# Moving two attention context groups within the software pipeline of a macaron layer

## The reference

```python
x = x + 0.5 * ffn(layernorm(x), k0, k1, k2, s0, s1, s2)
x = x + attn(layernorm(x), Wq, bq, Wk, bk, Wv, bv, gamma, beta)
x = x + 0.5 * ffn(layernorm(x), k0, k1, k2, s0, s1, s2)

# ffn: three dense layers with weights of +1 or -1 (128 -> 512 -> 512 -> 128),
#      h = relu(s * (h @ w)) * 2 between them
# attn: 16 heads of 8 features, softmax over 256 keys,
#       layernorm(context + x) * gamma + beta
```

## Time and profile before

| | us |
|---|---|
| median of 3 runs | 710.48 |
| lowest and highest | 710.31, 711.82 |
| profiled execution | 712.18 |
| its span, first to last instruction | 710.4 |
| busy: TensorE, VectorE, ScalarE, GpSimd | 672.6, 618.8, 488.0, 474.8 |

### The profile page before, as it was taken

How to read it: one execution, slowest core, us unless ns; L and a number is a source line. 1 busy time by engine, 2 the same in 40 slices (tenths; PEclk the granted TensorE clock), 3 DMA queues, 4 the chain that set the end, 5 groups by cost and what they waited for, 6 DMA issues and landing times. The chain is left out here.

```text
span 710.4 us, 18522 instructions
## 1 busy us (share of the span) xinstructions
PE 672.6 (95%) x7183; PEld 316.1 (45%) x7183; DVE 618.8 (87%) x1229; ACT 488.0 (69%) x704; POOL 474.8 (67%) x789
## 2 busy tenths in 40 slices
PE   7889989999999999999999999999999998888887
PEld 3434343444444444444434444444444444343436
DVE  6778888899899899989999989989989998887766
ACT  3436767777777777777776777777777777777743
POOL 5556477697777868687786869777786876254330
PEclk9999999999999999999999999999999999999999
DMA  3131221212221222122221221221222220110000
GB/s 85 31 60 54 61 70 31 69 48 61 57 44 56 60 70 62 52 63 53 49 57 58 61 70 47 61 63 38 63 53 69 47 59 28 46 41 2 18 1 30
DMA packets 72821, 36.38 MB, mean 51 GB/s; under 512 B 47648, under 2 KB 72736, under 8 KB 72736
## 3 DMA queue, kind: packets, MB, share of 16 engines
q1 hardware_dynamic: 71120, 34.49, 19.2%
q10 hardware_dynamic: 1616, 0.72, 0.4%
HBM read 5.05 MB, written 4.19 MB: 13 GB/s over the span
## 5 line engine op out<-in xcount | busy, mean ns | idle before, releaser
L1321 ACT ACTIVATE probs<-ps_t,score_scale 128x1024 f32<-128x1024 f32 x252 | 279.6, 1109 | 102.0 <-PE ps_t L998 99.6
L1673 DVE TENSOR_REDUCE row_max<-ps_s 128x4 f32<-128x1024 f32 x256 | 311.0, 1215 | 20.4 <-PE ps_s L985 20.1
L1545 DVE SCALAR_TENSOR_TENSOR ffn_lo<-ps_z,ffn_hi 128x512 f16<-128x512 f32 x232 | 157.9, 685 | 39.9 <-ACT ffn_hi L1279 37.7
L859 PE MATMUL ps_z<-ffn_hi,w 128*128 128x512 f16 x464 | 177.0, 382 | 0.5 <-DVE ffn_lo L1545 0.4
L860 PE MATMUL ps_z<-ffn_lo,w 128*128 128x512 f16 x464 | 175.9, 379 | 0.0
L1279 ACT ACTIVATE ffn_hi<-ps_z 128x512 f16<-128x512 f32 x232 | 137.1, 592 | 38.8 <-PE ps_z L849 20.6
L1038 PE MATMUL ps_c<-probs,v_cols 128*32 128x256 f32 x2048 | 131.0, 384 | 1.1 <-ACT probs L1321 0.7
L985 PE MATMUL ps_s<-k_rows,q_rows 32*128 32x256 f16 x1024 | 100.2, 273 | 18.0 <-DVE row_max L1673 15.7
L998 PE MATMUL ps_t<-q_rows,k_rows 32*128 32x256 f16 x992 | 97.1, 273 | 0.0
L1038 PEld LDWEIGHTS ps_c<-probs,v_cols 128*32 128x32 f32 x2048 | 56.7, 109 | 54.7 <-issue 27.0
L985 PEld LDWEIGHTS ps_s<-k_rows,q_rows 32*128 32x128 f16 x1024 | 28.9, 92 | 114.3 <-DVE row_max L1673 76.1
(11 more groups left out here) (224 smaller groups left out, 1085.1 us busy)
## 6 DMA issues: line engine op xcount, KB each, us to landing
x<-L_attn_x SPq DMA_DIRECT2D x16, 256.0 KB, 2.9
q_rows<-q_hi SPq DMA_DIRECT2D x32, 128.0 KB, 2.1
k_rows<-k_hi SPq DMA_DIRECT2D x31, 128.0 KB, 2.1
y<-x SPq DMA_DIRECT2D x15, 256.0 KB, 2.2
q_rows<-no_max SPq DMA_DIRECT2D x16, 128.0 KB, 2.1
q_rows<-q_lo SPq DMA_DIRECT2D x16, 128.0 KB, 2.1
k_rows<-k_lo SPq DMA_DIRECT2D x15, 128.0 KB, 2.1
q_rows<-max_rows SPq DMA_DIRECT2D x64, 8.0 KB
```

Of the source, the lines that this page charges most:

```text
L859: pe.matmul(o[:], w, ffn_hi[:, 1 + k, :], start=(k == 0), stop=False)
L1321: a_.activation(probs[n % PROBS][:, j:j + 2, :], o[:], ACT.Exp, scale=score_scale[:, 0:1]).then_inc(s_exp, 1)
L1545: v.scalar_tensor_tensor(out=ffn_lo[:, use, :], in0=z_bank(f, use)[:], scalar=0.0, in1=ffn_hi[:, use, :], op0=ALU.max, op1=ALU.subtract).t ...
L1673: v.tensor_reduce(row_max[hb % 2][:].rearrange("p (a l) e -> p l a e", a=2)[:, j:j + 2, :, g % 2], ps_s[:].rearrange("p l (a k) -> p l a k ...
```

## The change

The third and fourth context groups of each half are both taken at the step of the second scores. In numbers: groups 2 and 3 move from steps 3 and 4 to step 2, groups 6 and 7 from steps 19 and 20 to step 18. TensorE and ScalarE both read this table. It is used in iterations 1 to 14; iteration 15 has a table of its own. Within the step the contexts still stand behind the scores and ahead of the maxima's transposition and the network's piece.

```diff
-AT_CONTEXT = {0: (0, 1), 3: (2,), 4: (3,), 16: (4, 5), 19: (6,), 20: (7,)}
+AT_CONTEXT = {0: (0, 1), 2: (2, 3), 16: (4, 5), 18: (6, 7)}
```

## The result

The changed kernel takes 732.97 us in the median of four runs, 711.15 us before: a ratio of 1.0298 (95% interval 1.0282 to 1.0313). By the ratio that is 21.2 us more; the two medians are 21.8 us apart, the spans of the two profiled executions 20.9 us (731.3 and 710.4 us). 730.0 us and a range of 720.5 to 733.0 us were predicted, so the median lies 0.03 us inside the range's upper end.

A forecast was written before the change was run, and what follows sets the result against it. TensorE's order was taken to bound the kernel; 25 halves at 0.755 us (18.9 us) plus 0.6 us for iteration 1 gave 19.5 us on 710.48 us, so 730.0 us, range 720.5 to 733.0 us.

The forecast's parts named there:

- What bounds the kernel: Iterations 2 to 13: TensorE's order sets the time, VectorE 3.4 us per iteration behind; idle gaps opening on TensorE cost in full.
- Part 1: TensorE's own work, step 2 to m3: nothing saved by busy time, six turns per half kept, 0.11 us of waiting goes.
- the layout: New order placed on the old clock from the scores of step 2: m3 at 361.04, step 6 0.76 us late.
- Part 2: Banks of ps_z: m3 and the first middle product wait for remainders; 0.755 us per half, 18.9 us over 25 halves.
- The signs in the profile: Two new TensorE waits for remainders, about 0.4 and 0.3 us in 25 halves, some 17 us in all; iteration 42.0 us.
- the same layout: Half starting at step 16: same order and spacing as the first half, so step 22 comes 0.75 us late.
- Part 3: What else moves: context copy costs nothing, iteration 1's second half 0.6 us, iteration 14 nothing.
- (a): Rival: bank round trip covered, so only the wait before step 4 goes; 707.7 us, or 702.7 with turns saved; chance 0.06.
- (b): Rival: only the link from m1 to m3 binds, 0.27 us per half, 717.9 us; chance 0.10.
- (c): Rival: gain and stall cancel, no change, 710.5 us; chance 0.04.
- (d): Rival: TensorE's granted clock falls to 0.50 after the new gaps once per iteration, 15 us more, 745 us; chance 0.02.
- Busy time of TensorE unchanged: Expected sign in the profile after: TensorE's busy time stays the same despite the new waits.

The follow-up runs named there:

- the run with the late copy: Changed kernel with ScalarE's copy of the second context pair left at steps 4 and 20: 734.0 us, 1.032 of the kernel before the change.
- the run with the norm at step 21: Changed kernel with VectorE's mean and variance for the next network at step 21, not 20: 732.02 us, 1.0293 of the kernel before the change.
- fourth context only: Kernel before the change with only groups 3 and 7 moved, to steps 3 and 19: 728.48 us, ratio 1.0241.

## Why the prediction was right, and where it was off

- **What bounds the kernel.** Right. The new waits of TensorE came out in the time in full, and no later part of a half took any of them up: the starts of the scores are a constant distance from those of before from step 8 to the end of the half. The one exception is the second half of iteration 13, where an old wait took up a part: before, step 20 to step 22 took 3.18 us there (2.73 in the others), so it lost 0.52 us and not 0.85.
- **Part 1.** Right: contexts together save TensorE nothing. m1 starts at 2.20, scores 4 at 3.48, where the layout had 2.20 and 3.49 us behind step 2. The full array's turn in front of the transposition is there (370.88 to 371.19, 0.31 us), so the count of turns stayed at six, as the rows said against a reading of the contexts alone.
- **Part 2.** Right in mechanism and in each link: m3 at 4.22 (4.21), the first middle product at 4.96 (4.96), step 6 at 6.10 (6.10), step 8 at 8.26 (8.27). The first half's 0.74 us were predicted as 0.76. The signs in the profile were partly off: the waits for remainders come to 12.2 us in the list (8.9 + 3.3), not some 17, because the brackets leave out the tails of matmuls, and the gap at the first middle product has one in second halves only. That the banks are the cause, and not TensorE's order, is shown by the runs that hand them back sooner; that the fourth context was the cover of m2's and m1's banks, by those that move one context each.
- **The second half** was mis-sized: 0.75 us predicted, 0.85 measured. The step that failed is that "the same layout" holds there. Two waits more on VectorE stand in front of m2's remainder at step 20, and they cost 0.1 us. The trace of before had it, in rows that I did not put among mine: in the second half VectorE started m2's remainder 0.13 us after ScalarE's end, where the layout used the 0.03 us of m0's. Over the 11 second halves of iterations 2 to 12 this is 1.0 us. Iteration 13's second half lost 0.23 us less than predicted, and the first halves 0.01 us less each, so the 24 halves lost 18.75 us where 18.1 had been counted.
- **Part 3.** Iteration 1's second half lost 0.59 us (0.6). Iteration 14 lost 0.08 us (0): its first half gained 0.12 us and its second lost 0.20. The copy of the context pair was harmless, as the run with the late copy shows. By its rows it ends at 359.54; 359.42 is where ScalarE can go on, which changes nothing, since m1's result is there at 359.63.
- **The sum.** From the start of iteration 1 to the end the change costs 0.74 + 0.59 + 18.75 + 0.08 = 20.2 us in the profiled executions, against 19.5. The remaining 0.8 us of the 20.9 us between the spans arose ahead of iteration 1, where the edit doesn't act: 1.3 us more in iteration 0, at a lower granted clock, and 0.5 us less before it. Three of the four runs of the changed kernel have the mean clock of the profiled one, 0.995, and they are the ones near 733; the fourth, at a clock of 1.00, took 731.03 us, 20.7 us more than runs of before at 1.00 (710.3). The prediction expected 731.7 us for the like of the profiled execution and took off 1.7 us for the median. The profiled one took 733.12 us, and this deduction did not come: the median is 732.97 us. So the 3.0 us between 730.0 and the median are 0.7 us of mis-sized terms, 0.8 us from ahead of iteration 1, and most of the 1.7 us. The mechanism was right, but that the median stayed inside the range by 0.03 us was luck: which runs have the lower clock decided it. Whether the change makes such runs more frequent is not shown.
- **The rivals.** (a) would have had m3 0.33 us behind the scores of step 4; it came 0.74 us behind. (b), that only the first link binds, fell with the first middle product and the row maximum, which bind too. (c) fell with the time. (d): the granted clock in the steady iterations stayed at 1.00.
- "Busy time of TensorE unchanged" was wrong, 678.4 for 672.6 us: of these 5.8 us, 0.45 us per steady iteration (40.60 of 42.10 us, 40.15 of 40.50 before) is the tails in front of new gaps.

Here is the same iteration's row of the changed kernel by stretches (columns as in rows 2):

```profile
366.00:408.10 42.10, 40.60 (x448) 18.65 (x440) 37.38 (x73) 30.38 (x43) 30.68 (x51) 1.00 0.23 58
```

## What to carry to other kernels

Work that stands between a product and the next use of its bank is cover, whatever it computes: before moving it, add up how long the bank is away (here 0.6 us of matmuls, 0.6 and 0.7 us on the two engines that empty it) and see what is left between the two uses. Lay the new order out on the old clock engine by engine, and carry it on past the first wait: with two waits taken away, the next one here still cost 0.3 us a half. Compare each hand-over that the layout uses with the row of the very instruction that it stands for. A gap is worth what the next start is late, not the idle time in the bracket.

## What the runs showed of the hardware

- Two further waits on semaphores already reached, at the head of a step, put VectorE's next instruction 0.1 us later when it waits for ScalarE: 0.13 us after ScalarE's end instead of 0.03 (0.04 in the run with the norm at step 21).
- An idle bracket of TensorE is short of the real delay: by 0.07 us behind scores and at step 26 (0.34 for 0.41 us at m3, 0.24 for 0.31 us at step 26), and by 0.15 us behind a network product (0.55 for 0.70 us at the first middle product, fourth context only; in the changed kernel's first half 0.30 us with no bracket at all).
- In iterations 0 and 1, where TensorE is often idle, the granted clock drops for a few us in some executions and not in others. Runs of the same program differ in it: of 13 runs of before in one comparison, eight took 710.2 to 710.7 us at a mean clock of 1.00 and five 711.7 to 712.1 us at 0.998. The two rows are 50 to 60 us of the profiled executions of before and of the changed kernel, in which the edit has not yet acted: 1.00 against 0.83 (a mean over the 10 us; in the second, network products of 0.38 us are up to 0.63 us long), and the scores of step 16 came 0.77 us later.

```profile
50.00:60.00 10.00, 8.37 (x60) 2.68 (x64) 9.54 (x17) 4.92 (x8) 7.13 (x11) 1.00 0.15 28
```

```profile
50.00:60.00 10.00, 8.63 (x50) 2.52 (x48) 8.38 (x16) 4.18 (x7) 7.13 (x11) 0.83 0.15 28
```
